# Gathers that wait on counts, and last-layer weights transposed inside the sorted layer of a three-layer decoder

## What is computed

```python
x = x + attn(_layernorm(x))                        # 8 heads, sequences of 64
x = x + xattn(_layernorm(x), ctx)                  # below
x = x + ffn(_layernorm(x))

def _L0_xattn_ref(x, context, Wg, bg, W1, b1, W2, b2):       # E = 8, K = 2, FFN = 512
    logits = jnp.einsum('bsd,de->bse', context, Wg) + bg
    scores_topk, idx_topk = jax.lax.top_k(logits, K)
    weights = jax.nn.softmax(scores_topk, axis=-1)
    combine = jnp.sum(jax.nn.one_hot(idx_topk, E, dtype=weights.dtype) * weights[..., None], axis=-2)
    h = jax.nn.relu(jnp.einsum('bsd,edf->bsef', x, W1) + b1)
    y = jnp.einsum('bsef,efd->bsed', h, W2) + b2
    out = jnp.einsum('bsed,bse->bsd', y, combine)
    return out

def _L0_ffn_ref(...):                               # E = 32, I = 64, H = 128, top 8 by groups
    g = jax.nn.silu(jnp.einsum('th,eih->tei', h, w_gate))
    u = jnp.einsum('th,eih->tei', h, w_up)
    routed = jnp.einsum('tei,ehi->th', g * u * combine[:, :, None], w_down)
    sg = jax.nn.silu(h @ sh_gate.T)
    shared = sg * (h @ sh_up.T) @ sh_down.T
    return (routed + shared).reshape(B, S, Hd)
```

## Time and profile before

| | before |
|---|---|
| device time, median of 3 runs | 712.8 us (710.53 to 713.17) |
| span of the profiled execution (first to last instruction) | 713.0 us |
| own time of the profiled execution | the page gives its span alone |
| PE busy | 644.1 us, 90% |
| DVE busy | 529.1 us, 74% |
| ACT busy | 419.0 us, 59% |
| POOL busy | 352.7 us, 49% |
| mean granted clock of PE | 0.963 of full speed |
| HBM read and written | 64.48 and 18.87 MB |

### The profile page before, as it was taken

One profiled execution on the slowest core, in us unless ns is written; L12 is line 12 of the kernel. 1 busy time (PEld: TensorE's weight loads), 2 busy tenths in 40 slices (PEclk: granted clock), 3 DMA queues, 4 the chain that ended last, 5 costly groups with the idle time before them and its releaser, 6 DMA issues.

```text
span 713.0 us, 11540 instructions
## 1 busy us (share of the span) xinstructions
PE 644.1 (90%) x3538; PEld 486.2 (68%) x3538; DVE 529.1 (74%) x1337; ACT 419.0 (59%) x774; POOL 352.7 (49%) x418
## 2 busy tenths in 40 slices
PE   8878878886689999999976889999999999999997
PEld 8555555554577888888765556678686877777773
DVE  4787767777516666666673667899999999998973
ACT  3774656663219999999852444465564738374630
POOL 6135767678875555665347447273563728000000
PEclk9998989999999999999998989999999999999999
DMA  7930120000133676775111563454455546344561
GB/s 195 315 129 1 53 86 30 27 34 31 46 114 120 206 214 200 200 203 159 45 61 30 119 151 88 122 138 119 125 130 140 135 104 162 96 134 116 137 178 29
DMA packets 74875, 84.18 MB, mean 118 GB/s; under 512 B 15345, under 2 KB 43995, under 8 KB 74814
## 3 DMA queue, kind: packets, MB, share of 16 engines
q1 hardware_dynamic: 69688, 74.93, 37.4%
q0 software_dynamic: 4288, 8.40, 3.9%
q10 hardware_dynamic: 838, 0.11, 0.1%
HBM read 64.48 MB, written 18.87 MB: 117 GB/s over the span
## 4 chain that ended last, share of the span: by engine, by line
PE 51%; issue 21%; DVE 9%; ACT 4%; another core or an unknown queue 2%; POOL 2%; SPq 1%; DMA 1%; DVEq 0%; ACTq 0%
PE bank L1544 9%; PE bank L1546 8%; PE bank L1545 8%; PE pair_banks L1786 5%; PE pair_banks L1446 4%; PE score_banks L1546 3%; PE score_banks L1544 3%; PE score_banks L1545 3%; DVE t_s L1371 2%; PE pair_banks L1546 1%; PE pair_banks L1544 1%; PE pair_banks L1545 1%; DVE rc_s L1358 1%; POOL yg L660 1%
## 5 line engine op out<-in xcount | busy, mean ns | idle before, releaser
L931 ACT ACTIVATE r_s<-bank 128x512 f32<-128x512 f32 x136 | 80.7, 594 | 68.1 <-PE bank L1546 63.0
L1371 DVE TENSOR_TENSOR t_s<-rc_s,bcb 128x512 f32<-128x512 f32 x128 | 89.0, 698 | 4.7 <-PE pair_banks L1786 4.7
L660 POOL DMA_INDIRECT yg<-y_sorted,posi x64 | 70.2, 1096 | 30.8 <-issue 18.4
L577 POOL DMA_INDIRECT x_sorted<-xsb,posi x64 | 63.9, 998 | 32.5 <-DVE xsb L1162 17.4
L1358 DVE TENSOR_TENSOR rc_s<-r_s,score_banks 128x512 f32<-128x512 f32 x90 | 61.1, 679 | 20.7 <-ACT r_s L931 19.4
L1544 PE MATMUL bank<-fxh,Gh 128*128 128x512 f32 x136 | 73.8, 542 | 0.0
L707 ACT ACTIVATE t_h<-t_s 128x512 fp32r<-128x512 f32 x72 | 45.3, 629 | 42.5 <-DVE t_s L1371 28.2
L1786 PE MATMUL pair_banks<-t_s,Dn 128*128 128x512 f32 x128 | 63.3, 592 | 0.6 <-DVE t_s L1366 0.6
L1249 DVE TENSOR_TENSOR h1l<-score_banks,h1h 128x512 fp32r<-128x512 f32 x46 | 31.8, 691 | 31.5 <-ACT score_banks L877 31.5
L1414 DVE TENSOR_TENSOR t_l<-t_s,t_h 128x512 fp32r<-128x512 f32 x72 | 54.7, 759 | 0.2
L1546 PE MATMUL bank<-fxh,Gl 128*128 128x512 f32 x136 | 54.2, 398 | 0.0
(11 more groups left out here) (326 smaller groups left out, 1914.4 us busy)
## 6 DMA issues: line engine op xcount, KB each, us to landing
bcb<-c_rows SPq DMA_DIRECT2D x128, 256.0 KB
wraw<-in_L_xattn_W SPq DMA_DIRECT2D x46, 256.0 KB
x_sorted<-wraw SPq DMA_DIRECT2D x1, 5888.0 KB, 17.9
xg<-x_sorted SPq DMA_DIRECT2D x23, 256.0 KB, 3.2
y_sorted<-ysb SPq DMA_DIRECT2D x23, 256.0 KB, 2.5
ctxb<-in_ctx SPq DMA_DIRECT2D x8, 256.0 KB, 5.7
out<-x_all SPq DMA_DIRECT2D x8, 256.0 KB
x_all<-in_x SPq DMA_DIRECT2D x2, 512.0 KB, 5.4
```

Source lines behind the costliest of these rows:

```text
L577: pool.indirect_dma_start(out=xs, out_offset=bass.IndirectOffsetOnAxis(ap=posi[:, m, c:c + 1], axis=0), in_=xsb[:, m % SC, :], in_offset=N ...
L660: pool.indirect_dma_start(out=yg[:, j % 2, t, c, :], out_offset=None, in_=ys, in_offset=bass.IndirectOffsetOnAxis(ap=posi[:, j * TPS + t, ...
L931: act.activation(r_s[:, n % RB2, :], bank[n % 3][:, :], ACT.Silu).then_inc(F["act"], 1)
L1371: tt(t_s[:, n % TB2, :], rc_s[:, n % CB2, :], bcb[:, p - 1, :], ALU.mult).then_inc(F["t"], 1)
```

## The change

Two things are changed, with what they need.

1. *Counts.* The router works out how many stores of even and of odd blocks hold rows (`usedf`, times 16), and writes it as integers (`usedi`). POOL reads the two numbers into registers, waits for the two store semaphores up to those numbers, with a small operation behind each wait, and then issues the gathers of both first tiles, 16 in a row, before the reciprocal root. The rest of `y_sorted` (blocks 16 to 22) is filled with zeros at the start, and DVE waits for all stores before its loop of the last layer. The tiles `r_s`, `rc_s`, `t_s`, `t_h` and `t_l` are moved to the front of the last layer's space.
2. *Transposes within the sorted layer.* Group g of the raw weights is loaded at block g + 2, with two semaphores in turn and a wait for the load two before it; PE transposes it at the end of block g + 5 into bank 7 (`turn_f2`), and DVE alone makes its high and low halves in the next block, behind the first `h1l` (`split_f2`). The token transposes that come next wait for that split, since they use bank 7 too. ACT's copies and the old loops in the passage are gone.

```diff
+            pool.wait_ge(s_eb, 1)
+            stored = [pool.value_load(usedi[0:1, k:k + 1], min_val=16 * (NROW // 2), max_val=16 * ((NBK + 1) // 2))
+                      for k in range(2)]
+            for k in range(2):
+                pool.wait_ge(s_y[k], stored[k])
+                pool.tensor_tensor(turn[:, k:k + 1], mhalf[:, 0:1], mhalf[:, 0:1], ALU.mult)
-            pool.wait_ge(s_y[0], 16 * ((NBK + 1) // 2))
-            pool.wait_ge(s_y[1], 16 * (NBK // 2))
...
-            for t in range(TPS):
-                gather(0, t)
-            gather(1, 0)
+            for j in range(2):
+                for t in range(TPS):
+                    gather(j, t)
             rstd(0)
-            for t in range(1, TPS):
-                gather(1, t)
...
+            sp.dma_start(ys_v[NROW:NBK].rearrange("b p t d -> p b (t d)"),
+                         wraw[:, WB - 1, 0, :].unsqueeze(1).to_broadcast([P, NBK - NROW, F1])).then_inc(s_zero, 16)
...
             def load_raw(g):
+                if g >= RAWS:
+                    sp.wait_ge(s_late[g % RAWS], raw_landed(g - RAWS))
...
-                if 4 <= b < 4 + NG:
-                    load_raw(b - 4)
+                if 0 <= b - RAW_AT < NG:
+                    load_raw(b - RAW_AT)
...
+                ch.done(ts(in_use[:, 0:NBK], blk[:, :], ninc[:, E1 - 1:E1], 16.0, ALU.is_lt, ALU.mult))
+                ch.done(dve.tensor_reduce(usedf[:, :], in_use[:, :].rearrange("p (b k) -> p k b", k=2), AX.X, ALU.add))
+                dve.tensor_copy(usedi[:, :], usedf[:, :])
...
+            def split_f2(g):
+                dve.wait_ge(s_f2ps, g + 1)
+                halves = [(hi, lo, part) for hi, lo, part in f2_dst(g) if lo is not None]
+                if g in (9, 10, 11):
+                    at = slice((g - 9) * 4, (g - 8) * 4)
+                    halves.append((Dh[:, at, :], Dl[:, at, :], slice(0, 4)))
+                for hi, lo, part in halves:
+                    ins = dve.tensor_copy(hi, f2_bank()[:, part, :])
+                if halves:
+                    ch.done(ins)
+                for hi, lo, part in f2_dst(g):
+                    if lo is None:
+                        ins = dve.tensor_copy(hi, f2_bank()[:, part, :])
+                for hi, lo, part in halves:
+                    ins = tt(lo, f2_bank()[:, part, :], hi.bitcast(F32), ALU.subtract)
+                ins.then_inc(s_f2l, 1)
...
+                if c == 0 and 0 <= b - 1 - TURN_AT < NG:
+                    split_f2(b - 1 - TURN_AT)
...
             def to_tokens1(b):
                 pe.wait_ge(B["yT"], b + 1)
                 if b >= 1:
                     pe.wait_ge(B["ysb"], b)
+                if 0 <= b + 1 - TURN_AT < NG:
+                    pe.wait_ge(s_f2l, b + 2 - TURN_AT)
...
+            def turn_f2(g):
+                pe.wait_ge(s_late[g % RAWS], raw_landed(g))
+                pe.wait_ge(B["ysb"], g + TURN_AT - 1)
+                for c in range(4 if g < NG - 1 else 3):
+                    ins = transpose(f2_bank()[:, c, :], f2_raw(g)[:, c, :])
+                ins.then_inc(s_f2ps, 1)
...
+                if c == 3 and 0 <= b - TURN_AT < NG:
+                    turn_f2(b - TURN_AT)
```

More of the change, by code:

```diff
@@ L44 @@
 NCB = NBK * FB
+NROW = 2 * T // ST
 E2, I2 = 32, 64
@@ L50 @@
 NP = 6
-FB2 = (0, 1, 4, 5)
+RAWS, RAW_AT, TURN_AT = 2, 2, 5
 SCALE2 = 2.5
@@ L199, in decoder_kernel @@
         ebi = sb("ebi", [P, NBK], I32)
+        usedi = sb("usedi", [P, 2], I32)
+        turn = sb("turn", [P, 2])
         wraw = sb("wraw", [P, WB, 2, F1])
@@ L231, in decoder_kernel @@
             ebf = sb("ebf", [P, NBK])
+            in_use = sb("in_use", [P, NBK + 1])
+            usedf = sb("usedf", [P, 2])
             tri = sb("tri", [P, P])
@@ L283, in decoder_kernel @@
             a = allocator(st)
+            r_s = a("r_s", [P, RB2, ST])
+            rc_s = a("rc_s", [P, CB2, ST])
+            t_s = a("t_s", [P, TB2, ST])
+            t_h, t_l = (a(n, [P, HB2, ST], F32R) for n in ("t_h", "t_l"))
             Gh, Gl = (a(n, [P, NC2, P], F32R) for n in ("Gh", "Gl"))
@@ L323, in decoder_kernel @@
         s_xin = [sem(f"x_in{i}") for i in range(3)]
-        s_late = sem("f2_weights_in")
+        s_late = [sem(f"f2_weights_in{i}") for i in range(RAWS)]
         s_ctx = [sem(f"ctx_in{i}") for i in range(NQ)]
@@ L369, in f2_dst, with f2_bank, raw_landed @@
                     for n, (hi, lo) in enumerate(((Gh, Gl), (Uh, Ul), (Dn, None)))]
-        def f2_bank(g):
-            return bank[FB2[g % 4]][:, :].rearrange("p (a b) -> p a b", a=4)
+        def f2_bank():
+            return bank[7][:, :].rearrange("p (a b) -> p a b", a=4)
+        def raw_landed(g):
+            return 16 * (g // RAWS + 1) if g < NG - 1 else 16 * (g // RAWS + 3)
         def f2_raw(g):
@@ L574, in scatter @@
                     pool.wait_ge(s_pos, 1)
-                    pool.wait_ge(s_zero, 16)
+                    pool.wait_ge(s_zero, 32)
                 for c in range(2):
@@ L914, in acc_out @@
                 copy(accS[:, :], bank[6][:, :]).then_inc(F["accS"], 1)
[L916 to L920, removed]
             act.activation(warm[:, :], one[:, :], ACT.Sigmoid)
@@ L974, in _ @@
             dve.memset(cum[:, 0:1], 0.0)
+            dve.memset(in_use[:, NBK:NBK + 1], 0.0)
             dve.memset(bq[KR - 1:KR, :], 1.0)
@@ L1250, in _ @@
                     .then_inc(B["hl"], 1)
[L1253 to L1261, removed]
-                else:
-                    dve.wait_ge(s_f2h, g + 1 if g < 8 else 12)
-                    for hi, lo, part in f2_dst(g):
-                        if lo is not None:
-                            ins = tt(lo, f2_bank(g)[:, part, :], hi.bitcast(F32), ALU.subtract)
-                ins.then_inc(s_f2l, 1)
+                if c == 0 and 0 <= b - 1 - TURN_AT < NG:
+                    split_f2(b - 1 - TURN_AT)
             pc = Chain(dve, F["chain"])
@@ L1418, in _ @@
             halves = [m for some in halved.values() for m, _ in some]
+            dve.wait_ge(s_y[0], 16 * ((NBK + 1) // 2))
+            dve.wait_ge(s_y[1], 16 * (NBK // 2))
             for i in range(NS):
@@ L1743, in _ @@
                     to_tokens1(b - 2)
-            pe.wait_ge(s_late, 16 * (NG - 1 + 3))
-            for g in range(NG):
-                if g >= 4:
-                    pe.wait_ge(s_f2l, g - 3)
-                for c in range(4 if g < NG - 1 else 3):
-                    ins = transpose(f2_bank(g)[:, c, :], f2_raw(g)[:, c, :])
-                ins.then_inc(s_f2ps, 1)
+                if c == 3 and 0 <= b - TURN_AT < NG:
+                    turn_f2(b - TURN_AT)
             halves = [m for some in halved_at().values() for m, _ in some]
```

12 lines of the change are left out of this document (4 added, 8 removed).

## The result

| | before | after |
|---|---|---|
| device time, median (4 runs each, side by side) | 711.66 us (709.05 to 713.17) | 734.65 us (732.74 to 735.43) |
| ratio, 95% interval | | 1.0305 (1.0273 to 1.0336) |
| span of the profiled execution | 713.0 us | 733.6 us |

The forecast was 730 us with a range of 721 to 738. The kernel is slower by 23.0 us by the medians and by 20.6 by the two spans. In all other runs the time of the profiled execution is 1.8 us above its span (735.43 and 733.6 in after), so before's took some 714.8 us, an estimate from that offset: 3.1 us above its median, where after's is 0.8 above. That is the difference between 20.6 and 23.0.

What follows compares the result with a forecast made beforehand. PE was taken to pace the sorted layer, POOL the passage. Loop + 25.9 us, less POOL's wait, with counts, gathers and root, put logits 17.1 later; with 0.2 for the router, 713.0 + 17.3 gave 730 us, range 721 to 738.

Steps and rivals of the forecast that it cites:

- The bound and the sign: PE paces the sorted layer, so its added work and waits lengthen the kernel one for one; slower, chance 0.86.
- The pairs: Sorted layer, groups 0 to 7: copy and subtraction on DVE stall PE 1.5 us, plus 0.44 of transposes; 15.5 us.
- the hidden split: Rival in the sorted layer: DVE's split ends before PE's token transposes, only 5.6 us stay; 710 us, chance 0.11.
- Groups 8 to 12: Sorted layer: group 8, 0.44 + 0.8 us; groups 9 to 11, 0.44 + 2.1 each; group 12, 0.33 + 1.3.
- The sign given for these blocks: Blocks 6 to 18: token transposes 8.2 to 8.9 us apart, PE waiting 1.4 to 2.2 us for DVE's split.
- PE's stalls of 1.5 us should leave its clock alone.: Sorted layer: the new waits cost no clock, since PE was part idle at 357 to 359 with granted clock 1.00.
- The rival: Clock falls in the loop through the new stalls: 13 blocks grow by 60 us, near 785 us; chance 0.02.
- The counts: Passage: POOL's 12.35 us wait for the last stored block goes, less 1.4 us for reading two counts and gating.
- the lower bound that the prediction named: Passage, POOL: reading two counts into registers costs 0 if the reads run beside the last weight split.
- The six gathers ahead of the root: Passage, POOL: sixteen gathers stand before the reciprocal root where ten did; six at 1.26 us cost 7.6 us.
- Root to logits, 4.6 us: Passage end: 9.8 us shrinks to 4.6, the 5.2 us late PE signal going because gathers land before the root.
- start: Attention layer: three small router operations on DVE add 0.2 us, between 0 and 2.0.

Runs made afterwards that it cites:

- three runs above: Against after: transposes and split both earlier, 1.0049 and 1.0004 of before; transposes alone earlier, 1.0281; split alone ahead of the next block's first h1l, 1.0073.
- the split covered: After with PE's transposes a quarter block earlier and DVE's split behind that same quarter's h1l; 1.0049 of before on chip 0, 1.0004 on chip 9.
- the covered kernels: After with the split covered: root behind sixteen gathers, 1.0049 and 1.0004 of before; behind ten, 0.9973 and 0.9874; ten with all blocks awaited, 1.0117.
- the root behind ten: The split covered, with POOL's root after ten gathers in place of sixteen; 0.9973 of before on chip 0, 0.9874 on chip 9.

## Why the prediction was right, and where it was off

- **The bound and the sign.** These were right. The loop is paced by PE, what PE waits there lengthens it one for one, and the passage could not give it back.
- **The pairs.** The mechanism was right (three runs above), the size low: 2.15 us a block against 1.94. PE went on 4.47 us behind the product's start (294.33 − 289.86) and not 4.26, since the h1l came 0.1 later behind it than in the earlier trace rows and the handovers cost more than the 0.1 put down for them; PE was ready at 2.84 and not 2.73, its first pass behind transposes being 0.09 longer. So the stall was 1.63 and not 1.53. The other 0.1 is PE's own share, 0.5 us a group and not 0.44; with the split covered it is 0.5 to 0.6, and about 1 us with three operations, so that even the hidden split costs 8.4 us and not the 5.6 of its rival.
- **Groups 8 to 12.** From token transposes to token transposes their blocks grew by 1.4, 2.7, 2.7, 2.7 and 3.5 us against 1.2, three times 2.5, and 1.6. PE's wait for group 12 was as forecast (1.25 against 1.3). The excess of the last block (346.28 to 356.07) is the clock. The sign given for these blocks, 8.2 to 8.9 us, holds for the eight pairs alone: group 8 has 7.8, the others 9.1 and 9.8.
- **"PE's stalls of 1.5 us should leave its clock alone."** This held for those of 1.5 us, not for those of 2.05 us that the same sum had put there. The rival was right in kind and far too large: some 3.4 us at 0.50 and about 1.6 us lost, where it had 60 (and 730 + 60 is 790, not 785). The trace of after on chip 0 has the same fall behind the same wait (341.13); the covered kernels have none in the loop.
- **The counts.** The release is worth 12.3 us, forecast 12.35. Their price was 0.86 us, not 1.4: SP's register read of the earlier trace rows was a poor neighbour. The trace doesn't show POOL's reads; with 0.11 us between its last split and the gates, they most likely run beside that split, the lower bound that the prediction named.
- **The six gathers ahead of the root.** 7.6 us forecast. The covered kernel has 7.5 us less to the logits with the root behind ten on chip 0 (16.7 against 9.2) and 9.3 on chip 9. In time it is 5.3 and 9.3 by the ratios, 7.0 and 6.0 by the spans.
- **Root to logits, 4.6 us.** It measured 6.4: the signal was no longer late, but PE's fillers were slow instead. The reason given, gathers in flight, did not stand. The late signal stands in no trace of the 696 us chip, which has 3.0 to 4.2 us here in its eight traces. So the passage's gain on the first traces was partly luck: 5.2 us of it is a delay of before's execution that the change was not made to remove.
- **Behind the logits.** Nothing was forecast, and it is 2.0 us less: the second signal was 0.9 us less late, and the first products ran at full clock (0.23 us apart in place of 0.43).
- **In sum.** + 17.3 forecast; loop + 4.4, start 0.3 against 0.2, counts − 0.5, root to logits + 1.8, rest − 2.0, and small ones (− 0.5) make + 20.6 by the spans. Misses of both signs cancel in part here. On the 696 us chip, where before has no late signal to lose, the same change costs 3.6%, 25 us.

What DVE has free in a block was read as 2.2 us, and the hidden split was given 0.11. The covered kernels show that this time can be used, only not at the place where the change puts the split.

## What to carry over

When work is moved under a bound engine, ask where in the helper's order it lands: the same 1.4 us of DVE cost 2.15 us, 1.0 us or 0.55 us a block at three places of the same queue, PE's own 0.5 us in each (for the third, PE's transposes moved too). When two edits each remove one of two delays that run side by side, each alone shows nothing; price the pair, and run both alone before either is thrown away. A stage of which the trace has one execution on one chip should be seen on another before a gain is built on it.

## What was not expected of the hardware

- Chips differ by 16 us on the same kernel: before takes 713.1 us on chips 2 and 9, and 696.2 to 696.5 on chip 0. By the spans of before's first trace and of its trace on chip 0, 7.5 us lie ahead of the first `ysb`, 6.2 in the passage, and 4.1 behind the logits; the loop itself is equal to 0.02 us.
- In the six traces of before's time near 713 us (chips 2 and 9, and the two without a number), PE's fillers start in places 0.7 us and multiples of it apart in the passage, and a signal of PE in the second tile of the last layer comes 3.5 to 6.1 us late; in one of the six a signal of the first tile does too, by 5.2 us. In the eight traces of chip 0 neither is seen, and ACT reads the second tile's logits within 0.1 us of PE's end. All kernels had gathers in flight there on every chip, so these alone are not the cause. The cause stays open.
- A wait of 2.05 us in an otherwise full loop was followed by 3.4 us at the lower clock in some blocks and not in others (337.20 has the same wait and no fall behind it), and the waits of 1.5 us never were, in five traces with eight of them each. What decides it wasn't tried.
